# A causal-attention and ternary-FFN layer: wider and later turning of the row maxima, another order in the last projection, and weights rounded between a rope pair's products and sums

## The chip, the cores and the metric

The kernel runs on one core of one Trainium2 chip. The time is that of the device, in microseconds (us), from one launch to its end; lower is better. The names of the engines in what follows: PE is TensorE (matrix products), PEld its weight loads, DVE is VectorE, ACT is ScalarE, POOL is GpSimd, and SP (SyncE) issues the transfers.

## What is computed

For x of 8 batches x 512 tokens x 512 features, all in float32:

```
xn = layernorm(x)
q, k, v = xn @ Wq.T, xn @ Wk.T, xn @ Wv.T            # 16 heads of 32
q, k = rope(q), rope(k)
scores = q @ k.T / sqrt(32), causal
s = softmax(scores) @ v @ Wo.T
bitlinear(x, w) = absmax_quant(layer_norm(x)) @ (sign(round(w / gamma)) * gamma).T,  gamma = mean(|w|) (+ eps)
g = silu(bitlinear(gelu(bitlinear(xn, w_fc)), w_proj))   # 512 -> 2048 -> 512
out = x + s * g
```

## The kernel before

Each engine has one program, written out by hand, and semaphores join them; nothing is reordered by a scheduler. The batches run one after the other. In a batch PE does, in this order: the v products; the q and k products in four pairs (`qk`, L429); the output projection of the batch before; the 16 up-products of the FFN (L555); 44 rounds of scores; and last the 16 heads with transposed scores (L662), and the products with v (L681, `weigh`).

**The rounds.** A round is a row tile and one, two or four heads. `score_round` writes the scores into a PSUM bank (L534) and adds the causal mask (L541). DVE takes the row maxima (L1150), POOL (in the first rounds DVE) makes the bias, ACT takes exp with its row sum (L862). Rounds 4, 15, 26 and 37 hold four heads of the first row tile: there DVE subtracts the maxima (L1158), ACT takes exp (L854), and DVE sums two rounds later (L1164). Five PSUM banks go round, so round r waits until round r-5 has been summed (for round 26: until L1164, which round 31 waits for). Between the rounds PE does the down-products of the FFN (L600), and late output projections. How many is set by `GIVEN` (`FIRST_GIVEN` in batch 0), a table worked out from `EXP_COLS`, which counts 400 columns more for each round in `LSE_AFTER`. The down-products are six halves (h = 0 to 5) in banks 7, 5, 6, 7, 5, 6, and a last one in bank 7 (L611). ACT copies each half out (L875).

**The maxima.** While the second half of the heads is still in its rounds, DVE works out log-sum-exp of the first half (`lse_from_guess`, four steps of three small operations, one after each round in `LSE_AFTER`) and splits it in three f16 parts in `max_parts`, 24 columns for each row tile. After round `TURN_AFTER` PE transposes it (`turn_lse`, L574, four transposes) into the bank of down half `turned_in`; after round `MAX_COPY_AFTER` DVE copies it to `maxT` (L1078, which counts `maxT_ready`); SP moves it into three rows of `q_stack` (L364), and head 0 of the last stage waits for it (`max_dma`). The same happens for the other half of the heads in the last stage, after head 4's scores. The product that next uses the bank waits for `maxT_ready`. In the kernel before, `turned_in` is 6 in batch 0 and 5 in the other batches:

```python
if h == turned_in:
    pe.wait_ge(maxT_ready, 2 * b + 1)
...
if turned_in == N_HALF:
    pe.wait_ge(maxT_ready, 2 * b + 1)
```

**The first batch.** The weights of the FFN are made ternary on the way: the sum of magnitudes of each matrix (`absolute_sum` on DVE, L979, `sum_magnitudes` on ACT, L762), added over partitions by PE (`add_magnitudes`, L415), scales (`ffn_scales`), rounding in 16 units (`round_weights`, L953), turning by PE (`turn_weights`, L400) and keeping by ACT (`keep_weights`, L738 and L741). Rope on DVE has, for each pair, four products (L1126) and two sums (L1132). Hidden activations are made by L831 (gelu), L1172 and L1174.

**The end.** In the last batch `last_out_projection` (L467) makes the projection of the four token tiles after the last group of heads; `finish_context` (L1239, L1241) on DVE gives it that group, `finish_gate` (L1245) makes the gate, and `scale_by_gate` multiplies (L1086) and adds x (L1091).

Of the kernel before, what the change touches and what calls it, by code (L numbers as in the profile page):

```python
# [33 lines left out]
LSE_AFTER = {27: 0, 29: 1, 31: 2, 33: 3}  # L34
TURN_AFTER = 36
MAX_COPY_AFTER = 37
# [39 lines left out]
ABS_ACT = 3  # L76
# [33 lines left out]
def program(nc, x, w_q, w_k, w_v, w_o, w_fc, w_proj, rope_cos, rope_sin, out, norm_row):  # L110
    with ExitStack() as ctx:
# [32 lines left out]
        max_parts = mix[:, 0, 64:160].bitcast(F16).rearrange("p (a i s h) -> p a i s h", a=2, i=NT, s=SPLITS)  # L144
# [116 lines left out]
        TURNS_AFTER_QK = [[8, 9], [10, 11], [], [], fu[0:2], fu[2:3], fu[3:4], fu[4:5]]  # L261
        TURNS_IN_UP = {0: fu[5:7], 1: fu[7:8], 2: fu[8:10], 3: fu[10:11], 4: fu[11:12], 6: fu[12:13], 7: fu[13:14], 8: fu[14:15], 9: fu[15:16]}
        MADE_AFTER_ROPE = [fu[0:2], fu[2:5], fu[5:8], fu[8:12]]
        MADE_AFTER_UP = {3: fu[12:13], 4: fu[13:14], 5: fu[14:15], 6: fu[15:16]}
        PROJ_SUMS_BEFORE_ROPE = [(), (0, 1, 2), (3, 4), ()]
        KEPT_BEFORE_ROPE = [[], fu[0:2], fu[2:5], []]
        KEPT_IN_UP = {0: fu[5:7], 1: fu[7:8], 2: fu[8:10], 3: fu[10:11], 4: fu[11:12], 6: fu[12:13], 7: fu[13:14], 8: fu[14:15], 9: fu[15:16]}
# [120 lines left out]
        def _(pe):  # L388
# [82 lines left out]
            def last_out_projection(b):  # L471

                pe.wait_ge(ctx_lo, b * NG + NG - 1)
                for t in range(NT):
                    last_out_products(b, t, range(1 if t < NT - 1 else 0, NG - 1))
                pe.wait_ge(ctx_lo, b * NG + NG)
                for t in range(NT):
                    last_out_products(b, t, range(NG - 1, NG)).then_inc(wo_ps, 1)

            def body(b, first=False, last=False):  # L480
# [17 lines left out]
                for pair in range(4):  # L498
                    if pair >= 2:
                        pe.wait_ge(rope_prod_ready, b * 16 + 4 * (pair - 2) + 4)  # L500
                    if first:
                        pe.wait_ge(w_kept, ND + 2 * pair + 2)
                    for half in range(2):
                        three_products(banks[:, 2 + 2 * (pair % 2) + half, :],
                                       lambda a, r, c: (qkT[:, pair // 2, r, c, pair % 2, half, :], xT[:, a, c, :]),
                                       ND, "qk").then_inc(qk_ps, 1)
                        for u in TURNS_AFTER_QK[2 * pair + half] if first else []:
                            turn_weights(u, u + 1)
                        if first and (pair, half) == (1, 0):
# [34 lines left out]
                for f in range(FC):  # L544
# [12 lines left out]
                    mm.then_inc(fc_ps, 1)  # L557
                    for u in TURNS_IN_UP.get(f, []) if first else []:
                        turn_weights(u, u + 1)
                    if first and f == 0:  # L560
                        add_magnitudes(1)
# [8 lines left out]
                def turn_lse(half, bank):  # L570

                    pe.wait_ge(lse_split, 2 * b + half + 1)
                    for i in range(NT):
                        mm = pe.transpose(banks16[0:SPLITS * HH, bank, i * P:(i + 1) * P],  # L574
                                          max_parts[:, half, i].rearrange("p s h -> p (s h)"), ident16[:])
                    mm.then_inc(maxT_ps, 1)
# [152 lines left out]
        def _(act):  # L729
# [57 lines left out]
            def body(b, first=False, last=False):  # L787
# [15 lines left out]
                for pair in range(3):  # L803
                    for k in PROJ_SUMS_BEFORE_ROPE[pair] if first else []:
                        sum_magnitudes(1, k)
                    for n, u in enumerate(KEPT_BEFORE_ROPE[pair] if first else []):
                        keep_weights(u)
                        if pair == 2 and n == 1:
                            for k in range(5, N_ABS):
                                sum_magnitudes(1, k)  # L810
                    for u in OUT_KEPT_BEFORE_ROPE[pair] if b == 1 else []:
                        keep_weights(u)
                    split_rotated(pair)

# [87 lines left out]
        def _(dve):  # L902
# [79 lines left out]
            def first_weights():  # L982
# [21 lines left out]
                for k in range(ABS_ACT, N_ABS - 2):  # L1004
                    absolute_sum(k)
# [7 lines left out]
                for k in range(N_ABS - 2, N_ABS):  # L1013
                    absolute_sum(k)
                total_magnitudes(0)
# [98 lines left out]
            def body(b, first=False, last=False):  # L1114
# [4 lines left out]
                for pair in range(4):  # L1119
# [10 lines left out]
                    dve.wait_ge(rope_prod_ready, b * 16 + 4 * pair + 4)  # L1130
                    for half, op in enumerate((ALU.subtract, ALU.add)):
                        nc.vector.tensor_tensor(rope_sum[:, pair % 2, half, :], rope_prods[:, 2 * half, :], rope_prods[:, 2 * half + 1, :],  # L1132
                                                op).then_inc(rope_sum_ready, 1)
                    if pair == 0 and first:
                        ffn_scales(0)
                    if pair == 3 and first:
                        total_magnitudes(1)
                        ffn_scales(1)
# [109 lines left out]
                for g in range(NG):  # L1248
                    if g == 1 and not last:
                        normalise(b + 1)  # L1250
                    finish_context(g)
# [8 lines left out]
                for t in range(NT):  # L1260
                    finish_gate(t)
# [174 lines left out]
```

## Time and profile before

| | |
|---|---|
| time, median of 3 runs | 1143.91 us (1142.93 to 1144.2) |
| the profiled execution | 1143.62 us, span of its instructions 1141.9 us |
| granted TensorE clock, mean | 0.999 |
| busy: PE, DVE, ACT, POOL | 1104.4, 854.7, 793.4, 506.8 us |
| share of the chain that ended last | PE 86%, DVE 9%, ACT 3% |

The span runs from the first to the last instruction; the 1.7 us between it and the profiled time lie around it. PE is busy for 97% of the span, and a time saved on another engine counts only where PE waits for that engine.

### The profile page before, as it was taken

The numbers are of one execution on the slowest core, as the hardware profiler recorded it, in microseconds if no ns is written. First come the engines' busy times: TensorE is split into PE (matmuls) and PEld (weight loads), VectorE is DVE, ScalarE is ACT, GpSimd is POOL, SyncE is SP. The second block draws the span as 40 slices with busy tenths as digits, with TensorE's granted clock in tenths as the row PEclk, the third lists the DMA queues.
The fourth block names the chain that finished last, engine by engine and source line by source line (L and its number), as shares of the span: only waits on it lengthen the run. The fifth ranks groups of instructions, "written<-read, shape, count | busy, mean of one in ns | idle before, by whom it ended". The sixth has DMA issues, their size and how long they took to land.

```text
span 1141.9 us, 20209 instructions
## 1 busy us (share of the span) xinstructions
PE 1104.4 (97%) x7548; PEld 606.0 (53%) x7548; DVE 854.7 (75%) x1596; ACT 793.4 (69%) x1508; POOL 506.8 (44%) x915
## 2 busy tenths in 40 slices
PE   4989999999999999999999999999999999999997
PEld 3555654457444674446644475445744467444753
DVE  7997877798558986489756986479855897658964
ACT  4788884588835878269863798448882687727984
POOL 2135361563616635265433745156361653527533
PEclk9999999999999999999999999999999999999999
DMA  8391002920019101381016410192011910145111
GB/s 312 158 111 39 2 3 65 109 79 19 3 37 156 38 2 30 44 123 38 3 29 78 89 38 4 29 110 84 11 15 38 144 38 2 30 56 74 38 40 38
DMA packets 52610, 67.30 MB, mean 59 GB/s; under 512 B 9376, under 2 KB 34336, under 8 KB 52000
## 3 DMA queue, kind: packets, MB, share of 16 engines
q1 hardware_dynamic: 52512, 66.02, 31.4%
q8 instruction: 59, 0.97, 0.4%
q14 instruction: 39, 0.32, 0.1%
HBM read 31.98 MB, written 8.40 MB: 35 GB/s over the span
## 4 chain that ended last, share of the span: by engine, by line
PE 86%; DVE 9%; ACT 3%; issue 1%; DMA 1%; SPq 0%; POOL 0%; DVEq 0%
PE banks L429 21%; PE banks L555 19%; PE banks L600 11%; PE banks L662 7%; PE banks L681 7%; PE banks L534 5%; PE banks L611 5%; PE banks L446 5%; DVE mix L1150 2%; PE banks L541 2%; ACT banks L862 1%; PE banks L460 1%; DVE arena L1126 1%; PE banks L467 1%; DMA v_sb<-in_L_attn_Wv_dram 1%
## 5 line engine op out<-in xcount | busy, mean ns | idle before, releaser
L862 ACT ACTIVATE banks<-banks,mix,scl 128x384 f32<-128x384 f32 (+2 forms) x384 | 248.0, 648 | 26.9 <-POOL mix L1359 22.0
L1150 DVE TENSOR_REDUCE mix<-banks 128x1 f32<-128x512 f32 (+3 forms) x352 | 216.9, 636 | 34.2 <-PE banks L541 31.1
L555 PE MATMUL banks<-xT,fcT 128*128 128x512 f16 x1024 | 227.7, 379 | 2.1 <-ACT xh_buf L826 2.0
L600 PE MATMUL banks<-proj_ones,arena 128*128 128x256 f16 (+1 forms) x1536 | 214.4, 273 | 4.2 <-DVE mix L1078 4.2
L885 ACT ACTIVATE arena<-banks,scl 128x1280 f32<-128x1280 f32 x128 | 163.1, 1329 | 31.9 <-PE banks L662 29.0
L1350 POOL TENSOR_TENSOR xh_buf<-xh_buf 128x512 f32<-128x512 f32 x120 | 152.6, 1272 | 70.5 <-ACT xh_buf L826 69.2
L429 PE MATMUL banks<-xT,qkT 128*128 128x512 f16 x768 | 168.7, 379 | 0.0
L600 PEld LDWEIGHTS banks<-proj_ones,arena 128*128 128x128 f16 x1536 | 141.2, 97 | 41.6 <-issue 5.9
L555 PEld LDWEIGHTS banks<-xT,fcT 128*128 128x128 f16 x1024 | 98.5, 98 | 121.5 <-ACT xh_buf L826 6.8
L1359 POOL TENSOR_SCALAR mix<-mix,scl 128x1 f32<-128x1 f32 (+1 forms) x288 | 77.2, 268 | 183.3 <-DVE mix L1150 182.0
L1126 DVE TENSOR_TENSOR arena<-banks,mix 128x512 f32<-128x512 f32 x128 | 79.4, 682 | 93.6 <-PE banks L429 93.6
L831 ACT ACTIVATE banks<-banks,scl 128x512 f32<-128x512 f32 x128 | 84.8, 663 | 76.5 <-PE banks L555 75.3
L1344 POOL TENSOR_TENSOR xh_buf<-xr_buf,xh_buf 128x512 f16<-128x512 f32 x32 | 37.2, 1185 | 221.6 <-ACT xh_buf L801 221.6
L534 PE MATMUL banks<-stacks 96*128 96x384 f16 (+3 forms) x512 | 127.8, 300 | 4.5 <-DVE mix L1164 2.7
L1384 POOL TENSOR_SCALAR_AFFINE_SELECT arena<-arena 128x256 f32<-128x256 f32 x256 | 106.4, 444 | 43.0 <-ACT arena L885 39.6
L429 PEld LDWEIGHTS banks<-xT,qkT 128*128 128x128 f16 x768 | 74.9, 98 | 87.8
L1172 DVE TENSOR_SCALAR arena<-banks,scl 128x512 f16<-128x512 f32 x128 | 95.8, 748 | 27.3 <-ACT banks L831 26.5
L1174 DVE SCALAR_TENSOR_TENSOR arena<-banks,scl,arena 128x512 f16<-128x512 f32 x128 | 96.1, 751 | 4.5
L662 PE MATMUL banks<-stacks 99*128 99x512 f16 (+3 forms) x512 | 91.2, 301 | 0.0
L826 ACT ACTIVATE xh_buf<-banks,scl 128x512 f32<-128x512 f32 x128 | 87.3, 682 | 5.1 <-DVE arena L1174 3.2
L681 PE MATMUL banks<-arena,v_sb 128*32 128x512 f32 (+3 forms) x1024 | 87.0, 441 | 0.2 <-POOL arena L1384 0.2
L541 PE MATMUL banks<-mask_q,ident 128*128 128x128 bf16 (+2 forms) x352 | 85.8, 244 | 0.0
(165 smaller groups left out, 1450.8 us busy)
## 6 DMA issues: line engine op xcount, KB each, us to landing
stacks<-xh_buf SPq DMA_DIRECT2D x96, 128.0 KB, 5.2
stacks<-split_buf SPq DMA_DIRECT2D x96, 128.0 KB, 6.9
out_dram<-arena SPq DMA_DIRECT2D x32, 256.0 KB, 2.0
xr_buf<-in_L_attn_x_dram SPq DMA_DIRECT2D x7, 1024.0 KB, 9.9
resid<-in_L_attn_x_dram SPq DMA_DIRECT2D x28, 256.0 KB, 5.6
stacks<-in_L_ffn_w_fc_dram SPq DMA_DIRECT2D x1, 4096.0 KB, 25.4
arena<-in_L_ffn_w_proj_dram SPq DMA_DIRECT2D x1, 4096.0 KB, 15.3
mix<-norm_row SPq DMA_DIRECT2D x8, 256.0 KB, 4.9
```

Source lines behind the costliest of these rows:

```text
L429: mm = pe.matmul(out_ap, lhs, rhs, start=(c == 0 and k == 0), stop=(c == n - 1 and k == 2))
L534: pe.matmul(bank[:, k * keys:(k + 1) * keys], q_stack[0:KS, h0 + k, i * P:(i + 1) * P], k_stack[0:KS, h0 + k, 0:keys], start=(k == 0), sto ...
L541: pe.matmul(diagonal, ident16[:], mask, start=False, stop=True).then_inc(s_ps, 1)
L555: mm = pe.matmul(banks[:, UP_BANKS[f % NUB], :], fcT[:, c, f * P:(f + 1) * P], xT[:, part, c, :], start=(c == 0 and part == 0), stop=(c == ...
L600: mm = pe.matmul(banks[:, DOWN_BANKS[h % 3], 0:cols.stop - cols.start], hid[:, part, f, t * P:(t + 1) * P], proj_ones[:, f, cols], start=( ...
L662: mm = pe.matmul(ps[:, at:at + n], k_stack[0:KM, h, j * P:(j + 1) * P], q_stack[0:KM, h, j * P:S], start=True, stop=True)
L681: mm = pe.matmul(banks[k * DK:(k + 1) * DK, 6 + g % 2, j * P:S], v_sb[:, j, head * DK:(head + 1) * DK], probs[:, g % 2, k, at:at + n], sta ...
L862: mm = nc.scalar.activation(block, block, ACT.Exp, scale=col(EXP_SCALE), bias=exp_bias[:, i, h0 + k:h0 + k + 1], accum_out=row_sum[:, i, h ...
L885: nc.scalar.activation(probs[:, g % 2, h % GH, :], st_region[h % 2][:, 0:PROBS], ACT.Exp, scale=col(EXP_SCALE)).then_inc(probs_ready, 1)
L1150: nc.vector.tensor_reduce(row_max[:, i, h0:h0 + n], scores_of(r), AX_X, ALU.max).then_inc(max_ready, 1)
L1350: nc.gpsimd.tensor_tensor(sq_sum[:], sq_sum[:], squares[f % NSQ], ALU.add).then_inc(sq_added, 1)
L1384: nc.gpsimd.affine_select(blocks, blocks, [[0, 2], [1, P]], ALU.is_ge, 0.0, base=0, channel_multiplier=-1).then_inc(probs_masked, 1)
```

## The change

Four things are changed.

1. **Turning of the maxima, every batch.** `LSE_AFTER`, `TURN_AFTER` and `MAX_COPY_AFTER` move by one or two rounds, and `max_parts` moves to another place of `mix`, so that each transpose reads 128 columns (its own 24 and what stands behind them) in place of 24. `turned_in` becomes 6 in every batch. `GIVEN` is worked out from the new table.
2. **Last projection.** PE finishes tiles 0 and 1 before it starts tiles 2 and 3, and DVE finishes the gate before the last group's context in place of after it.
3. **First batch, DVE.** Units of weights are rounded between a pair's products and its sums; one of the five absolute sums of w_fc that DVE did goes to ACT; totals are taken behind the sums of pair 0, and ahead of those of pair 3.
4. **First batch, PE and ACT.** Units are turned and kept somewhat later.

```diff
-LSE_AFTER = {27: 0, 29: 1, 31: 2, 33: 3}
-TURN_AFTER = 36
-MAX_COPY_AFTER = 37
+LSE_AFTER = {28: 0, 30: 1, 32: 2, 34: 3}
+TURN_AFTER = 38
+MAX_COPY_AFTER = 39
-ABS_ACT = 3
+ABS_ACT = 4
-        max_parts = mix[:, 0, 64:160].bitcast(F16).rearrange("p (a i s h) -> p a i s h", a=2, i=NT, s=SPLITS)
+        parts_f = mix[:, 1, 304:452].bitcast(F16)
+        max_parts = parts_f[:, 0:8 * SPLITS * HH].rearrange("p (a i s h) -> p a i s h", a=2, i=NT, s=SPLITS)
-        TURNS_AFTER_QK = [[8, 9], [10, 11], [], [], fu[0:2], fu[2:3], fu[3:4], fu[4:5]]
+        TURNS_AFTER_QK = [[8, 9], [10, 11], [], [], [], fu[0:1], fu[1:3], fu[3:5]]
-        MADE_AFTER_ROPE = [fu[0:2], fu[2:5], fu[5:8], fu[8:12]]
+        MADE_BEFORE_SUMS = [[], fu[0:2], fu[3:5], fu[6:8]]
+        MADE_AFTER_ROPE = [[], fu[2:3], fu[5:6], fu[8:12]]
@@ last_out_projection
-                for t in range(NT):
-                    last_out_products(b, t, range(1 if t < NT - 1 else 0, NG - 1))
+                for t in range(2):
+                    last_out_products(b, t, range(1, NG - 1))
                 pe.wait_ge(ctx_lo, b * NG + NG)
-                for t in range(NT):
+                for t in range(2):
                     last_out_products(b, t, range(NG - 1, NG)).then_inc(wo_ps, 1)
+                for t in range(2, NT):
+                    last_out_products(b, t, range(1 if t < NT - 1 else 0, NG)).then_inc(wo_ps, 1)
@@ turn_lse
-                        mm = pe.transpose(banks16[0:SPLITS * HH, bank, i * P:(i + 1) * P],
-                                          max_parts[:, half, i].rearrange("p s h -> p (s h)"), ident16[:])
+                        at = (half * NT + i) * SPLITS * HH
+                        mm = pe.transpose(banks16[:, bank, i * P:(i + 1) * P], parts_f[:, at:at + P], ident16[:])
@@ first_weights (DVE)
-                for k in range(ABS_ACT, N_ABS - 2):
+                for k in range(ABS_ACT, N_ABS - 1):
                     absolute_sum(k)
 ...
-                for k in range(N_ABS - 2, N_ABS):
-                    absolute_sum(k)
-                total_magnitudes(0)
+                absolute_sum(N_ABS - 1)
@@ body (DVE)
+                    for u in MADE_BEFORE_SUMS[pair] if first else []:
+                        round_weights(u)
+                    if pair == 3 and first:
+                        total_magnitudes(1)
                     for half, op in enumerate((ALU.subtract, ALU.add)):
 ...
                     if pair == 0 and first:
+                        total_magnitudes(0)
                         ffn_scales(0)
                     if pair == 3 and first:
-                        total_magnitudes(1)
                         ffn_scales(1)
@@ last part of the batch (DVE)
+                    if g == NG - 1 and last:
+                        for t in range(NT):
+                            finish_gate(t)
                     finish_context(g)
 ...
-                for t in range(NT):
+                for t in range(0 if last else NT):
                     finish_gate(t)
```

On PE the place is rounds 37 to 39 of batch 1, the same in batches 2 to 7 (batches are counted from 0). `stacks` are the scores of a round, `mask_q` their mask, `proj_ones` the down-products (256 or 257 columns by half), `ident,mix` the turning of the maxima. Before, with the last down-products of round 36 as the first row:

```order
L600 MATMUL banks<-proj_ones,arena 128x256 x10
L574 MATMUL banks<-ident,mix 24x128 x4
L534 MATMUL banks<-stacks 128x128 x4
L541 MATMUL banks<-mask_q,ident 128x512
L600 MATMUL banks<-proj_ones,arena 128x256 x8
L534 MATMUL banks<-stacks 128x384
L541 MATMUL banks<-mask_q,ident 128x128
L600 MATMUL banks<-proj_ones,arena 128x256 x2
L600 MATMUL banks<-proj_ones,arena 128x257 x4
L534 MATMUL banks<-stacks 128x384
```

And in the changed kernel:

```order
L606 MATMUL banks<-proj_ones,arena 128x256 x6
L540 MATMUL banks<-stacks 128x128 x4
L547 MATMUL banks<-mask_q,ident 128x512
L606 MATMUL banks<-proj_ones,arena 128x256 x12
L540 MATMUL banks<-stacks 128x384
L547 MATMUL banks<-mask_q,ident 128x128
L606 MATMUL banks<-proj_ones,arena 128x256 x2
L606 MATMUL banks<-proj_ones,arena 128x257 x2
L581 MATMUL banks<-ident,mix 128x128 x4
L540 MATMUL banks<-stacks 128x384
```

The turning stood ahead of round 37, with 10 down-products between it and half 5 (the first row of 257 columns at this place), which uses its bank. Now it stands ahead of round 39, after half 5 has begun, in the bank that only the last product (L611 before) uses again, and its output has 128 rows in place of 24.

On DVE the place is the same batch from round 26 (`128x4` with the subtraction behind it) on. Before:

```order
L1150 TENSOR_REDUCE mix<-banks 128x4
L1158 TENSOR_TENSOR banks<-banks,mix 128x512
L1150 TENSOR_REDUCE mix<-banks 128x1
L1056 TENSOR_TENSOR mix<-mix 128x32
L1057 TENSOR_SCALAR mix<-mix 128x32
L1058 TENSOR_SCALAR mix<-mix 128x32
L1150 TENSOR_REDUCE mix<-banks 128x1
L1164 TENSOR_REDUCE mix<-banks 128x4
L1150 TENSOR_REDUCE mix<-banks 128x1
```

And in the changed kernel:

```order
L1163 TENSOR_REDUCE mix<-banks 128x4
L1171 TENSOR_TENSOR banks<-banks,mix 128x512
L1163 TENSOR_REDUCE mix<-banks 128x1 x2
L1177 TENSOR_REDUCE mix<-banks 128x4
L1065 TENSOR_TENSOR mix<-mix 128x32
L1066 TENSOR_SCALAR mix<-mix 128x32
L1067 TENSOR_SCALAR mix<-mix 128x32
L1163 TENSOR_REDUCE mix<-banks 128x1 x2
```

The three small operations of the first step stood ahead of round 28's maxima and of the sum of round 26 (`128x4`, L1164 before); now they stand behind both.

On DVE at the end of the program, before (`ctxT` is the last group's context, `gate_sum` the gate, `arena` the result):

```order
L1239 CAST ctxT<-banks 128x512
L1241 TENSOR_TENSOR ctxT<-banks,ctxT 128x512
L1245 SCALAR_TENSOR_TENSOR gate_sum<-xr_buf,gate_sum 128x512 x4
L1086 SCALAR_TENSOR_TENSOR arena<-banks,gate_scale,gate_sum 128x512 x2
L1091 TENSOR_TENSOR arena<-arena,xh_buf 128x512
```

And in the changed kernel:

```order
L1258 SCALAR_TENSOR_TENSOR gate_sum<-xr_buf,gate_sum 128x512 x4
L1252 CAST ctxT<-banks 128x512
L1254 TENSOR_TENSOR ctxT<-banks,ctxT 128x512
L1095 SCALAR_TENSOR_TENSOR arena<-banks,gate_scale,gate_sum 128x512 x2
L1100 TENSOR_TENSOR arena<-arena,xh_buf 128x512
```

The four operations of the gate changed places with the two of the context. On PE the 39 products at this end are the same in number, in another order of tiles.

## Rows read from the trace of the kernel before

**Rows 1.** The page, chain that ended last, shares of the span by engine.

```profile
PE 86%; DVE 9%; ACT 3%; issue 1%; DMA 1%; SPq 0%; POOL 0%; DVEq 0%
```

**Rows 2.** Waits of the whole span: us in total, times, longest.

```profile
PE banks L600 <- DVE mix L1078: 4.2, 7, 0.6
PE banks L534 <- DVE mix L1164: 2.7, 8, 1.1
```

**Rows 3.** Timeline of PE, batch 1: start, length, instructions [idle before <-releaser].

```profile
271.36 0.60 PE L600 MATMUL banks<-proj_ones,arena 128*128 128x256 f16 x4
272.19 0.39 PE L534 MATMUL banks<-stacks 96*128 96x256 f16 x2 [0.22 <-DVE mix L1164]
...
280.34 0.38 PE L600 MATMUL banks<-proj_ones,arena 128*128 128x256 f16 x2
...
281.32 0.60 PE L600 MATMUL banks<-proj_ones,arena 128*128 128x257 f16 x4 [0.60 <-DVE mix L1078]
```

**Rows 4.** Timeline of ACT and DVE, batch 1, rounds 26 to 28.

```profile
269.49 0.66 ACT L854 ACTIVATE banks<-banks,scl 128x512 f32<-128x512 f32 x1
...
269.83 0.18 DVE L1056 TENSOR_TENSOR mix<-mix 128x32 f32<-128x32 f32 x1
...
270.98 0.56 DVE L1150 TENSOR_REDUCE mix<-banks 128x1 f32<-128x384 f32 x1
...
271.45 0.68 DVE L1164 TENSOR_REDUCE mix<-banks 128x4 f32<-128x512 f32 x1
```

**Rows 5.** The chain in order of time, batch 1: start, us, work.

```profile
277.43 1.10 PE banks L600 x10
...
295.65 0.55 PE banks L662 x4
...
296.64 0.32 PE banks L574 x4
296.96 0.65 PE banks L662 x4
```

**Rows 6.** The same view, batch 0.

```profile
24.87 0.45 PE banks L403 x8
```

**Rows 7.** Groups by line and shape, weight loads of two kinds of transposes.

```profile
L403 PEld LDWEIGHTS banks<-ident,split_buf 128*128 128x128 f16 x96 | 7.1, 109 | 4.4 <-DVE split_buf L919 2.8 <-issue 0.2
...
L574 PEld LDWEIGHTS banks<-ident,mix 128*24 128x24 f16 x64 | 3.4, 92 | 5.1 <-issue 5.1
```

**Rows 8.** Timeline of batch 1, stage of the heads.

```profile
291.43 7.55 ACT L885 ACTIVATE arena<-banks,scl 128x1280 f32<-128x1280 f32 x6 [2.84 <-PE banks L662]
...
297.10 0.41 DVE L1078 COPY mix<-banks 24x512 f16<-24x512 f16 x1 [3.40 <-PE banks L574]
...
301.84 0.49 PEld L662 LDWEIGHTS banks<-stacks 99*128 99x128 f16 x4 [0.20 <-issue]
```

**Rows 9.** Timeline of the end of the program.

```profile
1123.22 2.55 ACT L892 ACTIVATE xr_buf<-gate_sum,gate_scale 128x512 f32<-128x512 f32 x4
...
1127.01 8.59 PE L467 MATMUL banks<-voT,ctxT 128*128 128x512 f16 x39
1127.15 0.69 DVE L1239 CAST ctxT<-banks 128x512 f16<-128x512 f32 x1 [2.85 <-PE banks L681]
...
1128.48 2.49 DVE L1245 SCALAR_TENSOR_TENSOR gate_sum<-xr_buf,gate_sum 128x512 f32<-128x512 f32 x4
...
1137.89 0.75 DVE L1086 SCALAR_TENSOR_TENSOR arena<-banks,gate_scale,gate_sum 128x512 f32<-128x512 f32 x1
```

**Rows 10.** Timeline of batch 0, projections.

```profile
42.15 2.34 DVE L979 TENSOR_REDUCE ln<-stacks 128x1 f32<-128x1024 f32 x2
...
47.95 1.22 ACT L801 CAST xh_buf<-xr_buf 128x512 f16<-128x512 f32 x2 [2.56 <-DVE xr_buf L1132]
...
71.09 0.16 DVE L937 TENSOR_SCALAR scl<-banks 128x1 f32<-128x1 f32 x1 [0.47 <-PE banks L415]
...
78.76 1.90 PE L555 MATMUL banks<-xT,fcT 128*128 128x512 f16 x8 [1.61 <-ACT xh_buf L826]
```

More of the change, by code:

```diff
@@ L260, in program @@
         TURNS_AFTER_V = [[4], [5], [6], [7]]
-        TURNS_AFTER_QK = [[8, 9], [10, 11], [], [], fu[0:2], fu[2:3], fu[3:4], fu[4:5]]
-        TURNS_IN_UP = {0: fu[5:7], 1: fu[7:8], 2: fu[8:10], 3: fu[10:11], 4: fu[11:12], 6: fu[12:13], 7: fu[13:14], 8: fu[14:15], 9: fu[15:16]}
-        MADE_AFTER_ROPE = [fu[0:2], fu[2:5], fu[5:8], fu[8:12]]
+        TURNS_AFTER_QK = [[8, 9], [10, 11], [], [], [], fu[0:1], fu[1:3], fu[3:5]]
+        TURNS_IN_UP = {0: fu[5:6], 1: fu[6:7], 2: fu[7:9], 3: fu[9:10], 4: fu[10:11], 5: fu[11:12],
+                       6: fu[12:13], 7: fu[13:14], 8: fu[14:15], 9: fu[15:16]}
+        MADE_BEFORE_SUMS = [[], fu[0:2], fu[3:5], fu[6:8]]
+        MADE_AFTER_ROPE = [[], fu[2:3], fu[5:6], fu[8:12]]
         MADE_AFTER_UP = {3: fu[12:13], 4: fu[13:14], 5: fu[14:15], 6: fu[15:16]}
-        PROJ_SUMS_BEFORE_ROPE = [(), (0, 1, 2), (3, 4), ()]
-        KEPT_BEFORE_ROPE = [[], fu[0:2], fu[2:5], []]
-        KEPT_IN_UP = {0: fu[5:7], 1: fu[7:8], 2: fu[8:10], 3: fu[10:11], 4: fu[11:12], 6: fu[12:13], 7: fu[13:14], 8: fu[14:15], 9: fu[15:16]}
+        PROJ_SUMS_BEFORE_ROPE = [(), (0, 1, 2, 3), (4,)]
+        KEPT_BEFORE_ROPE = [[], fu[0:1], fu[1:3]]
+        PROJ_SUMS_AFTER_KEPT = [(), (), (5,)]
+        KEPT_IN_UP = {0: fu[6:7], 1: fu[7:8], 2: fu[8:9], 3: fu[9:10], 4: fu[10:11], 5: fu[11:12], 6: fu[12:13], 7: fu[13:14], 8: fu[14:15], 9: fu[15:16]}
         OUT_TURNS_AFTER_QK = [[], ou[0:1], ou[1:2], ou[2:3], ou[3:4], [], [], []]
@@ L508, in body @@
                             turn_weights(u, u + 1)
-                        if first and (pair, half) == (1, 0):
+                        if first and (pair, half) == (1, 1):
                             add_magnitudes(0)
@@ L557, in body @@
                     mm.then_inc(fc_ps, 1)
+                    if first and f == 1:
+                        add_magnitudes(1)
                     for u in TURNS_IN_UP.get(f, []) if first else []:
                         turn_weights(u, u + 1)
-                    if first and f == 0:
-                        add_magnitudes(1)
                     if FC - EARLY <= f < FC - 1:
@@ L805, in body @@
                         sum_magnitudes(1, k)
-                    for n, u in enumerate(KEPT_BEFORE_ROPE[pair] if first else []):
+                    for u in KEPT_BEFORE_ROPE[pair] if first else []:
                         keep_weights(u)
-                        if pair == 2 and n == 1:
-                            for k in range(5, N_ABS):
-                                sum_magnitudes(1, k)
+                    for k in PROJ_SUMS_AFTER_KEPT[pair] if first else []:
+                        sum_magnitudes(1, k)
                     for u in OUT_KEPT_BEFORE_ROPE[pair] if b == 1 else []:
@@ L813, in body @@
                     split_rotated(pair)
+                if first:
+                    keep_weights(fu[3])
+                    for k in (6, 7):
+                        sum_magnitudes(1, k)
+                    keep_weights(fu[4])
+                    keep_weights(fu[5])
                 nc.scalar.preload_act_table(ACT.Gelu)
```

## The prediction, made before the changed kernel ran

> **What bounds the kernel now.** I read the chain that ended last first. PE holds 86% of the span in it [rows 1], so the question is where PE waits, and where it is slowed without a wait. The list of waits gives the first: among PE's waits two come back once in nearly every batch, one of 0.60 us for DVE's copy of the turned maxima (L1078, 7 times) and one for the sum of a four-head round (L1164, 8 times) [rows 2]. The timeline then shows what each really costs. Down-products follow each other every 0.11 us (10 in 1.10) [rows 5]. The two that start at 280.34 would let the next start at 280.56; it starts at 281.32: 0.76 us lost. The four that start at 271.36 would let round 31 start at 271.80; it starts at 272.19: 0.39 us lost [rows 3]. Batches 2 to 7 show the same two places with the same waits. Last, the chain in order of time shows work that takes longer than it should: after the turning of the maxima four score products hold 0.65 us, and 0.55 a head earlier, and the four transposes themselves hold 0.32 [rows 5].
>
> **The two waits of a round (change 1).** The bank of the turned maxima was that of down half 5, which came 10 down-products and two rounds after them. Now it is bank 7, which nothing uses until the last product after all rounds, so the wait of 0.76 us goes, in batches 1 to 7 (batch 0 had that bank already). The 0.39 us go if the sum of round 26 is ready by 271.80. DVE began the first log-sum-exp step at 269.83 and came to round 28's maxima only at 270.98 (0.56), then to the sum (0.68) [rows 4]. Without the step in between, the maxima run from 269.8 to 270.4, and the sum, whose input ACT had ready at 269.49 + 0.66 = 270.15 [rows 4], from 270.4 to 271.1: 0.7 us ahead of need. The step then runs where the sum was; DVE's work in the rounds is the same in sum, so all that follows on DVE is no later than before. Sum: 7 x (0.76 + 0.39) = 8.05 us. Below it the bound is nothing, if other waits take their place (a rival, below); above it there is none, since the waits can't give more than they cost.
>
> **The width of the transposes (change 1).** Four transposes of 128 columns at full pace take half of what eight take: 0.45 / 2 = 0.22 us, and behind those eight the v products come without delay [rows 6]. The turning holds 0.32, and the products behind it 0.10 more than usual [rows 5]: 0.20 us for each turning. I put this down to the 24-column weights, which seem not to be loaded beside the products ahead. There are 16 turnings; the first of batch 0 lies where DVE is behind, so 15 x 0.20 = 3.0 us. From below: no gain, and four loads each dearer by 109 - 92 = 17 ns [rows 7], 64 in all: 1.1 us lost. I take the 3.0, since the transposes of [rows 6] are of the same type and the very width that the change brings. A rule speaks against it. The Trainium skill (TensorE: Matmul & The Clock Gate, LDWEIGHTS) says that a load's time goes with its number of columns, about P / 1.2 ns; by it a load of 24 columns should take 20 ns and one of 128 107 ns, and 64 loads would cost 5.6 us more if nothing hid them. The trace doesn't bear it out for the narrow one: 92 ns against 109 [rows 7].
>
> **The last projection (change 2).** The 39 products begin at 1127.01 and take 0.22 us each [rows 9]. Before, the first tile was whole after 30 of them, at 1133.6, and DVE then had four tiles one behind the other and came to the last scaling at 1137.89 [rows 9]. Now tile 0 is whole after 15 (1130.3), tile 1 after 18, tile 2 after 27 (1132.9) and tile 3 after 39 (1135.6). With some 1.5 us of DVE's work for a tile, tiles 0 to 2 are done by about 1134.8, and the last scaling starts at 1135.75: 2.1 us earlier. The gate now stands ahead of the last context on DVE. It takes 2.49 us, and DVE waited 2.85 us ahead of the context's 1127.15, since 1124.3; the last tanh ends at 1123.22 + 2.55 = 1125.77 [rows 9], so the gate ends at about 1127.0 and fits. Were it late, the context would be too, but PE has 12 products (2.6 us) to do before it needs it, 1.2 us more than the context takes. So 2.1 us; bounds 1.5 and 2.3.
>
> **The first batch (changes 3 and 4).** DVE's two absolute sums of w_fc behind the rope rows, 2.34 us, become one: 1.17 us less [rows 10], at a place where PE and ACT both wait for DVE (1.61 us of PE's at 78.76, 2.56 of ACT's at 47.95) [rows 10]. The sum that ACT takes over costs it about as much, and that wait of 2.56 us covers it. The exchange over PE for the total (0.47 us idle of DVE at 71.09) [rows 10] goes for w_proj, where sums now stand in between, and comes for w_fc, which had the products of pair 0 in between: no change. Rounding between products and sums moves the same 12 units about, none is added; the units that are turned later were waiting for DVE before. Cover is the idle time of PE at 78.76; if it's gone, a turned unit costs PE some 1 us. I take 1.0 us of the 1.17, bounds 0 and 1.6. In the rounds of batch 0 DVE is the one that is behind, and there the copy (0.41 us, as in [rows 8]) no longer stands ahead of the sum of round 37: 0.4 us.
>
> **The sum.** 8.05 + 3.0 + 2.1 + 1.0 + 0.4 = 14.55 us. The profiled execution took 1143.62 us (span 1141.9, and 1.7 around it), so 1129.1; the median of the runs shown is 0.3 above it: **1129.3 us**.
>
> **Will the gain be kept?** At the end of the rounds ACT had waited 2.84 us for head 0's scores [rows 8]; with PE some 1.35 us earlier it still waits 1.5, so PE stays the one that decides. In the stages behind, everything hangs on PE's pace and moves with it.
>
> **Rivals.**
>
> A. *Other waits take the place of the two.* PE arrives earlier at rounds 32 to 41, while the banks come free by ACT's sums, which hang on DVE's maxima, and those come no earlier. For it: the room before each such bank is small, and the products between the rounds, which make it, now alternate (2, 4, 2, 4 of the counted pairs). Against it: no other wait of PE in the rounds of batches 1 to 7 is in the list. If half of 8.05 comes back, 1133.3; if all, 1137.4.
>
> B. *The wide transposes bring nothing, or cost.* The 0.20 us could come from the turning itself or from the f16 output. Then the sum loses 3.0 to 4.1: 1132.3 to 1133.4. By the Trainium skill's rule on loads, named above, it would be 1137.9.
>
> C. *Slower: the rows of maxima reach head 0 too late.* The copy of the first half now comes two rounds later, near 282, and SP's transfer must land before head 0's scores, which start 0.7 us ahead of 291.43 - 1.35, at 289.3: 7 us of room. For the second half the copy starts at 297.10 and PE begins head 8 with them at 301.84 [rows 8], so 4.7 us are enough. It would take a landing 2.1 us later than the room, 9 us, in all 8 batches to undo the 14.55 us and lose 0.2% (2.3 us); a landing after 10 us gives 1129.3 + 8 x 2.9 = 1152.
>
> D. *PE was not held by these waits:* what it gains it gives back ahead of the heads, in the wait for ACT's last sums. Then only the turnings and the tail could count, and, with the former lost too, the time stays within 0.2%. Against it stand the 2.84 us of ACT.
>
> **Numbers.** Main case 0.57, A 0.24, B 0.12, C 0.04, D 0.03. The range takes in the main case with its bounds (1128.5 with all upper ones, and 1.1 less if the longest wait for the sum, 1.1 us in batch 0 [rows 2], goes as well), B, and A to somewhat over half: 1127 to 1136. About 0.2%, 2.3 us, is what a measurement of this kernel can tell from no change. Faster 0.93, same 0.03, slower 0.04.
>
> **What would show it.** In the profile after: no wait of PE for the copy of the maxima and none for the sum of round 26 in batches 1 to 7; the four transposes at 0.22 us in the chain with 0.55 behind them; a batch shorter by 1.55 us; the last scaling 2.1 us nearer to PE's last part; the first hidden activation 1 us earlier. The prediction is wrong if PE shows new waits for ACT or DVE in rounds 32 to 41, or ahead of head 0; if the transposes still hold 0.32; or if rounding ahead of the sums delays the transfers of the rotated pairs so that the first scores wait.

## The result, and the profile after

| | before | changed |
|---|---|---|
| median | 1143.51 us (4 runs) | 1127.11 us (4 runs, 1124.74 to 1128.03) |
| ratio | | 0.9853, 95% interval 0.9836 to 0.9870 |
| the profiled execution | 1143.62 us, span 1141.9 | 1127.08 us, span 1125.4 |

The ratio is 16.8 us of 1143.51; the forecast was 14.6 us. By it the time is 1126.7 us, a little below the lower end of the range (1127.0), while the median itself is a little above it. So the direction and nearly all terms were right, and one was too small.

The page of the changed kernel, the chain that ended last, shares of the span by engine, which answers to [rows 1]:

```profile
PE 92%; DVE 3%; ACT 2%; POOL 1%; DMA 1%; issue 1%; SPq 0%; DVEq 0%; POOLq 0%
```

DVE went from 9% to 3% of it. In the waits of the changed kernel (us, times, longest) neither of [rows 2] is left for PE. Behind the opening one (12.5 us) and one of 2.1 us at 13.2 us, which stand in both kernels, the largest waits of its matmuls are these:

```profile
PE banks L561 <- ACT xh_buf L837: 2.7, 1, 2.7
...
PE banks L540 <- ACT banks L873: 2.0, 4, 0.8
```

The 2.7 us are new in size ([rows 10] had 1.61 at the same place, up-product 3 of batch 0). The others are the four of batch 0, where the kernel before had four too.

The chain in order of time, batch 1 of the changed kernel: the last down-products ahead of the first turning, the turning (L581) and the down-products behind it; then a head's scores ahead of the second turning, that turning and the scores behind it.

```profile
276.60 0.44 PE banks L606 x4
277.04 0.22 PE banks L581 x4
277.48 0.89 PE banks L606 x8
...
291.22 0.55 PE banks L668 x4
...
292.20 0.22 PE banks L581 x4
292.42 0.55 PE banks L668 x4
```

Against [rows 5] the four transposes hold 0.22 us in place of 0.32, and the scores behind them 0.55 in place of 0.65: 0.20 us for each turning, as forecast. The timelines show the weight loads of that second turning, first in the kernel before, then in the changed one:

```profile
296.57 0.22 PEld L574 LDWEIGHTS banks<-ident,mix 128*24 128x24 f16 x4 [0.43 <-issue]
```

```profile
291.82 0.43 PEld L581 LDWEIGHTS banks<-ident,mix 128*128 128x128 f16 x4
...
292.04 0.38 PE L581 MATMUL banks<-ident,mix 128*128 128x128 f16 x4
```

The down-products ahead end at 296.64 before and at 292.20 after. So the narrow loads began 0.07 us before that end, together with the transposes themselves (296.57), and the wide ones 0.38 us before it.

A measure for each batch is the first of the 32 products of one column behind the rounds (L635 before, L641 after). It starts at 149.27 us in batch 0 and at 1096.58 in batch 7 of the kernel before, and at 146.17 and 1082.52 in the changed one. Batch 0, in the kernel before and in the changed one:

```profile
149.27 0.94 PE L635 MATMUL banks<-ones,arena 128*128 128x1 f16 x32
```

```profile
146.17 0.94 PE L641 MATMUL banks<-ones,arena 128*128 128x1 f16 x32
```

So batch 0 gave 3.10 us up to there, the seven periods between them 14.06 - 3.10 = 10.96 us (forecast 10.85), and what lies behind it 16.5 - 14.06 = 2.4 us (forecast 2.1 and 0.2 of a turning). The middle and the end are as forecast; batch 0, where I had 1.4, is not. The measure of batch 0 carries the opening of the program with it, which differs by up to 1.2 us between profiled executions whose edits lie behind it. The periods between batches don't: from the third one on they are 134.92 us before and 133.37 after, each within 0.01 us.

The end of the program, timeline of the changed kernel, for [rows 9]:

```profile
1109.94 2.49 DVE L1258 SCALAR_TENSOR_TENSOR gate_sum<-xr_buf,gate_sum 128x512 f32<-128x512 f32 x4
...
1112.75 8.59 PE L471 MATMUL banks<-voT,ctxT 128*128 128x512 f16 x39
1112.88 0.69 DVE L1252 CAST ctxT<-banks 128x512 f16<-128x512 f32 x1 [0.45 <-PE banks L687]
...
1116.30 1.41 DVE L1095 SCALAR_TENSOR_TENSOR arena<-banks,gate_scale,gate_sum 128x512 f32<-128x512 f32 x2 [2.01 <-PE banks L471]
...
1121.38 0.75 DVE L1095 SCALAR_TENSOR_TENSOR arena<-banks,gate_scale,gate_sum 128x512 f32<-128x512 f32 x1 [0.90 <-PE banks L471]
```

The gate ends 0.45 us ahead of the context, and the last scaling comes 8.63 us behind PE's first product there, in place of 10.88: 2.25 us.

Batch 0, stretches of the changed kernel's time: us, then busy time of PE, PEld, DVE, ACT and POOL with instructions, granted TensorE clock, DMA share, GB/s.

```profile
70.00:72.00 2.00, 1.95 (x17) 1.67 (x15) 1.31 (x2) 2.00 (x5) 1.39 (x2) 1.00 1.15 116
72.00:74.70 2.70, 0.03 (x1) 0.03 (x2) 2.59 (x5) 1.42 (x3) 1.33 (x1) 1.00 1.25 73
74.70:78.00 3.30, 3.30 (x9) 1.23 (x10) 2.05 (x3) 2.08 (x3) 1.14 (x1) 0.51 1.17 124
```

PE sat idle for 2.7 us, and then the clock was granted at 0.51, the lower of its two levels (1.2 GHz), for 3.3 us. The length of the wait alone doesn't tell when this happens: a wait of 2.08 us that ended at 15.3 us, in both kernels, left the clock at 1.00. The eight products of up-product 3 show it in the timeline:

```profile
74.67 3.53 PE L561 MATMUL banks<-xT,fcT 128*128 128x512 f16 x8 [2.72 <-ACT xh_buf L837]
```

They took 3.53 us where the same eight took 1.90 in [rows 10]. Up-product 3 began 4.09 us earlier than before (78.76), and 1.6 us of that went to the clock. The run at 1124.74 us has a mean clock of 1.0 in place of 0.998.

Where did 4.09 us come from, when I had forecast 1.0 for the whole of changes 3 and 4? The groups of the 16 roundings, before:

```profile
L953 DVE TENSOR_SCALAR ctxT<-arena,scl 128x1024 f32<-128x1024 f32 x4 | 5.2, 1324 | 0.0
...
L953 DVE TENSOR_SCALAR gate_sum<-stacks,scl 128x1024 f32<-128x1024 f32 x4 | 4.4, 1122 | 0.0
...
L953 DVE TENSOR_SCALAR gate_sum<-arena,scl 128x1024 f32<-128x1024 f32 x4 | 3.8, 974 | 0.0
L953 DVE TENSOR_SCALAR ctxT<-stacks,scl 128x1024 f32<-128x1024 f32 x4 | 3.7, 973 | 0.0
```

and in the changed kernel:

```profile
L964 DVE TENSOR_SCALAR ctxT<-arena,scl 128x1024 f32<-128x1024 f32 x4 | 3.4, 862 | 0.7 <-PE banks L404 0.7
L964 DVE TENSOR_SCALAR ctxT<-stacks,scl 128x1024 f32<-128x1024 f32 x4 | 3.4, 876 | 0.2
L964 DVE TENSOR_SCALAR gate_sum<-arena,scl 128x1024 f32<-128x1024 f32 x4 | 2.9, 747 | 0.0
L964 DVE TENSOR_SCALAR gate_sum<-stacks,scl 128x1024 f32<-128x1024 f32 x4 | 2.9, 746 | 0.0
```

The same 16 operations took 17.1 us before and 12.6 after. The timeline of before shows which were slow: those beside a subtraction of POOL.

```profile
55.77 2.32 DVE L953 TENSOR_SCALAR ctxT<-stacks,scl 128x1024 f32<-128x1024 f32 x2
55.99 3.13 POOL L1344 TENSOR_TENSOR xh_buf<-xr_buf,xh_buf 128x512 f16<-128x512 f32 x2 [5.06 <-ACT xh_buf L801]
58.02 1.64 DVE L953 TENSOR_SCALAR gate_sum<-stacks,scl 128x1024 f32<-128x1024 f32 x1
...
64.03 1.41 DVE L953 TENSOR_SCALAR ctxT<-stacks,scl 128x1024 f32<-128x1024 f32 x2
...
67.28 2.72 POOL L1344 TENSOR_TENSOR split_buf<-xr_buf,split_buf 128x512 f16<-128x512 f32 x2 [8.16 <-ACT split_buf L801]
67.93 2.61 DVE L1132 TENSOR_TENSOR xr_buf<-arena 128x512 f32<-128x512 f32 x2
```

With POOL quiet (64.03) two roundings take 1.41 us; beside it one alone takes 1.64. The two rope sums at 67.93 take 2.61 us beside POOL. That was in the trace that I had, and I read it as a fixed duration.

The sum of DVE's work up to its first operation on hidden activations (L1172 at 76.44 before, L1185 at 72.36 after: 4.08 us) is this. Less: the 12 roundings ahead of it take 9.7 us in place of 12.75 (3.0; the rest of the 4.5 lies behind it), pair 3's rope sums 1.28 in place of 2.61 (1.3), the sum that went to ACT 1.1, and one small operation of the scales 0.18 in place of 0.82 (0.6). More: new waits of 0.47 for the total of w_fc, 0.70 more for that of w_proj, 0.69 for a turned unit and 0.17 for ACT, 2.0 in all. Three of the rows, from the timeline of the changed kernel:

```profile
65.13 1.28 DVE L1145 TENSOR_TENSOR xr_buf<-arena 128x512 f32<-128x512 f32 x2
67.58 0.16 DVE L948 TENSOR_SCALAR scl<-banks 128x1 f32<-128x1 f32 x1 [1.17 <-PE banks L419]
...
71.12 1.21 DVE L964 TENSOR_SCALAR ctxT<-arena,scl 128x1024 f32<-128x1024 f32 x1 [0.69 <-PE banks L404]
```

### The profile page after: what moved, and what is told of

Same layout as the page of the kernel before. It is cut to its first block, busy times and chain, and to the rows that moved or that the text cites. A ratio compares the mean times of both kernels' runs of the same rounds, so it can differ in the third digit from the quotient of the medians.

```text
span 1125.4 us, 20210 instructions
## 1 busy us (share of the span) xinstructions
PE 1100.0 (98%) x7548; PEld 609.2 (54%) x7548; DVE 843.7 (75%) x1595; ACT 791.3 (70%) x1510; POOL 503.7 (45%) x915
## 4 chain that ended last, share of the span: by engine, by line
PE 92%; DVE 3%; ACT 2%; POOL 1%; DMA 1%; issue 1%; SPq 0%; DVEq 0%; POOLq 0%
PE banks L433 23%; PE banks L561 20%; PE banks L606 14%; PE banks L687 7%; PE banks L668 7%; PE banks L540 6%; PE banks L450 5%; PE banks L617 4%; PE banks L547 2%; ACT banks L873 2%; PE banks L464 1%; PE banks L404 1%; PE banks L471 1%; DVE mix L1163 1%; DMA v_sb<-in_L_attn_Wv_dram 1%
## 5 line engine op out<-in xcount | busy, mean ns | idle before, releaser
L1185 DVE TENSOR_SCALAR arena<-banks,scl 128x512 f16<-128x512 f32 x128 | 95.9, 749 | 29.7 <-ACT banks L842 29.1
```

## Experiments

Each was timed in five rounds against the kernel before on the same chip. A gain in us is 1 less the ratio, times the time before.

**Change 1 alone** (`turning_only`).

```diff
-LSE_AFTER = {27: 0, 29: 1, 31: 2, 33: 3}
-TURN_AFTER = 36
-MAX_COPY_AFTER = 37
+LSE_AFTER = {28: 0, 30: 1, 32: 2, 34: 3}
+TURN_AFTER = 38
+MAX_COPY_AFTER = 39
...
+        parts_f = mix[:, 1, 304:452].bitcast(F16)
...
+                        mm = pe.transpose(banks16[:, bank, i * P:(i + 1) * P], parts_f[:, at:at + P], ident16[:])
```

> The kernel before with change 1 alone (later steps, later and wider turning). Theory (two waits and the narrow loads go, PE paces): 7 x 1.55 + 0.4 in batch 0's rounds = 11.3 us less, 1132.3; each batch from 2 on shorter by 1.56 us. Rival (the gain of the whole change came from elsewhere, or needs the first batch's changes): less than 8 us.

Measured: 1132.58 us, ratio 0.9902 (0.9888 to 0.9915), 11.2 us. The theory holds; most of the change's gain is here. A batch is shorter by 1.55 us (133.37 against 134.92), and the measure of batch 0 comes 0.64 us earlier (148.63).

**Its three parts, one by one.** Only the width (`wide_only`):

```diff
-        max_parts = mix[:, 0, 64:160].bitcast(F16)...
+        parts_f = mix[:, 1, 304:452].bitcast(F16)
...
-                        mm = pe.transpose(banks16[0:SPLITS * HH, bank, i * P:(i + 1) * P], ...
+                        mm = pe.transpose(banks16[:, bank, i * P:(i + 1) * P], parts_f[:, at:at + P], ident16[:])
```

> The kernel before with transposes of 128 columns in place of 24, and nothing else. Theory (0.10 us ahead of and 0.10 behind each turning is the price of the narrow loads): 15 to 16 turnings x 0.20 = 3.0 to 3.2 us less where PE paces; the first turning of a batch stands ahead of the wait for DVE's copy, which may take its part back: 1140.5 to 1142. Rival (the width is of no account or a wide load is dearer): 1143.5 to 1144.6.

Measured: 1141.34 us, 0.9977 (0.9968 to 0.9986), 2.6 us; a batch takes 134.52 us, 0.40 less. The changed kernel with the width alone undone (`narrow_after`, the same diff reversed):

> The changed kernel with transposes of 24 columns as before, and nothing else changed back. Theory: 15 x 0.20 = 3.0 us more than the changed kernel, 1130.1. Rival (width of no account): 1127.1.

Measured: 1129.66 us, 0.9877 (0.9863 to 0.9890). Against the 0.9853 of the changed kernel, 2.7 us more by the ratios, though the intervals of the two (each against before) overlap a little. The periods are sharper: 133.77 us against 133.37, 0.40 for two turnings. Both runs say that the narrow transposes cost what the chain showed, 0.20 us a turning. The edit also gives the output 128 rows and moves `max_parts`; no run parts these from the width of the weights. In the waits of this kernel the weight loads' idle time of [rows 7], 5.1 us in 16 pieces, is back in the same size:

```profile
PEld banks L579 <- issue: 5.1, 16, 0.4
```

Only the place of the turning and the copy (`turn_later_only`):

```diff
-TURN_AFTER = 36
-MAX_COPY_AFTER = 37
+TURN_AFTER = 38
+MAX_COPY_AFTER = 39
```

> The kernel before with the turning and its copy two rounds later, the steps of the log-sum-exp where they were, narrow transposes. Theory: the wait of PE for the copy goes, 7 x 0.76 = 5.3 us, and the 0.39 us for the sum of round 26 stays: 1138.2. Rival (the two waits stand for each other: the one left grows): 1140 or more.

Measured: 1138.74 us, 0.9955 (0.9942 to 0.9967), 5.1 us; a batch takes 134.16 us, 0.76 less. The wait for the copy is no longer in the list, and that for the sum of round 26 stands as it did in [rows 2]:

```profile
PE banks L534 <- DVE mix L1164: 2.7, 8, 1.1
```

Only the steps (`lse_only`). `GIVEN` and the bank of the turning in batch 0 are worked out from this table, so they move with it:

```diff
-LSE_AFTER = {27: 0, 29: 1, 31: 2, 33: 3}
+LSE_AFTER = {28: 0, 30: 1, 32: 2, 34: 3}
```

> The kernel before with the steps of the log-sum-exp one round later and nothing else. Theory: the 0.39 us for the sum of round 26 go, 7 x 0.39 = 2.7 us, and the turning, which now has two rounds in place of three behind the last step, doesn't wait: 1141.3. Rival (the wait for the copy grows by what the other gives): 1144.

Measured: 1141.32 us, 0.9978 (0.9969 to 0.9987), 2.5 us. The time is that of the theory, but by luck. The wait for the sum is gone; the one for the copy stays, with one long case in it and one short wait of a turning for the last step:

```profile
PE banks L600 <- DVE mix L1078: 3.0, 8, 1.9
...
PE banks L574 <- DVE mix L1070: 0.5, 1, 0.5
```

The long case is in batch 0; the other seven are short. Timeline of this kernel, batch 0 and batch 1:

```profile
147.01 0.82 PE L600 MATMUL banks<-proj_ones,arena 128*128 128x257 f16 x6 [1.92 <-DVE mix L1078]
...
282.88 1.48 PE L600 MATMUL banks<-proj_ones,arena 128*128 128x256 f16 x12
...
284.96 0.38 PE L600 MATMUL banks<-proj_ones,arena 128*128 128x257 f16 x2 [0.15 <-DVE mix L1078]
```

In batch 1 `GIVEN` now puts 14 down-products between the turning and half 5 (12 here, 2 behind the next round) in place of 10, and the wait for the copy falls from 0.60 to 0.15 us. So a batch takes 134.08 us, 0.84 less: 0.39 for the sum and 0.45 for the copy, 5.96 us over the seven periods. In batch 0 no down-product stands between the turning and the half in its bank. PE waits 0.55 and 1.92 us there, and the granted clock is 0.53 from 148 to 151 us. Batch 0 ends 4.48 us later for it (1.2 of them are from the opening). The mean clock was 0.997 in 9 of the 11 runs, against 0.998 to 0.999 before.

One by one the three parts shorten a batch by 0.40 + 0.76 + 0.84 = 2.00 us, together by 1.55. The two waits overlap by the 0.45 of the copy. That 2.6 + 5.1 + 2.5 = 10.2 us of the whole times comes near the 11.2 is only because `lse_only` loses in batch 0 what it gains too much in the others. What the two waits give together is seen in `narrow_after`: 134.92 - 133.77 = 1.15 us a batch, the 0.76 + 0.39 of the forecast.

**Change 2 alone** (`tail_only`), the diff of the last projection and of `finish_gate` as shown with the change.

> The kernel before with change 2 alone (order of the last projection, gate ahead of the last context). Theory: last scaling 2.1 us earlier relative to PE's last part, 1141.4. Rival (the stores at the end decide): less than 1 us.

Measured: 1141.82 us, 0.9981 (0.9972 to 0.9990), 2.2 us, as forecast.

**Changes 3 and 4 alone** (`first_only`): the changed kernel with changes 1 and 2 undone.

> The kernel before with changes 3 and 4 alone (first batch). Theory (what I left out is that rounding no longer runs beside POOL's subtractions, so that DVE's 16 roundings take 12.6 us in place of 17.1): PE's stages of batch 0 come 2.3 us earlier, up to 3.9 if the clock doesn't fall in the wait ahead of up-product 3: 1141.2, down to 1139.6. Rival (only the absolute sum that went to ACT counts, as I forecast): 1142.5.

Measured: 1141.04 us, 0.9975 (0.9966 to 0.9984), 2.9 us, against the 1.0 of my forecast (1.4 with the rounds, whose 0.4 belongs to change 1). In the profile batch 0 gives 2.42 us. The clock fell here too: up-product 3 waited 2.73 us and took 3.58.

**Rounding put back behind the sums** (`round_late`).

```diff
-        MADE_BEFORE_SUMS = [[], fu[0:2], fu[3:5], fu[6:8]]
-        MADE_AFTER_ROPE = [[], fu[2:3], fu[5:6], fu[8:12]]
+        MADE_BEFORE_SUMS = [[], [], [], []]
+        MADE_AFTER_ROPE = [[], fu[0:3], fu[3:6], fu[6:12]]
```

> The changed kernel, with the units rounded behind the sums of each pair again; all else as changed. Theory (contention with POOL): the roundings of pairs 1 to 3 run beside POOL's subtractions again and take some 4 us more in all, of which PE sees 1.5 to 3: 1129 to 1130. Rival (the place of the rounding is of no account, only the sum on ACT and the timetable of turning are): 1127, as the changed kernel.

Measured: 1129.24 us, 0.9874 (0.9860 to 0.9887), 2.4 us more than the changed kernel by the ratios, whose intervals overlap. The time is as the theory said, but not for its reason: the 16 roundings took 11.6 us, less than in the changed kernel. ACT came later to the cast that frees POOL: POOL started 3.6 us behind pair 1's sums in place of 0.1 in the kernel before, and now ran beside pair 2's rope sums. Timeline of this kernel, last the wait ahead of pair 3's sums:

```profile
55.71 2.73 POOL L1360 TENSOR_TENSOR xh_buf<-xr_buf,xh_buf 128x512 f16<-128x512 f32 x2 [6.54 <-ACT xh_buf L807]
...
56.65 2.35 DVE L1145 TENSOR_TENSOR xr_buf<-arena 128x512 f32<-128x512 f32 x2
...
65.28 0.16 DVE L938 TENSOR_REDUCE w_all<-ln 128x1 f32<-128x8 f32 x1 [1.79 <-ACT resid L768]
```

The sums took 2.35 us; in the changed kernel they take 1.28, and there POOL runs beside the rope products, which read PSUM and take 2.48 us with or without it, and beside one rounding (1.26). So it isn't the rounding's place as such that counts but what POOL meets, and what DVE has to do while it waits. Counted from the same operation (the rope rows, 40.61 here and 41.12 in the changed kernel) the first hidden activation comes 2.0 us later. The sums beside POOL are 1.1 of it; the wait for ACT's sums of w_proj, 1.79 us in place of 0.17, is 1.6; and a longer wait for a turned unit is 0.45. The faster roundings give back 1.0, and a shorter wait for the total 0.1. In the changed kernel two roundings fill the time in which DVE here waits for ACT.

**POOL kept away from the roundings** (`pool_waits`), all else as before.

```diff
                         pool.wait_ge(rot_hi_ready, b * 8 + 2 * pair + half + 1)
+                        if first:
+                            pool.wait_ge(w_unit_ready, n_first + (2, 5, 8, 12)[pair])
```

> The kernel before, but in batch 0 POOL starts the subtraction of each rope pair only when DVE has rounded the units that stand beside it (2, 5, 8 and 12 of them). Theory (roundings beside POOL's subtractions are slowed): the 16 roundings take about 12 us in place of 17.1, the first hidden activation comes 3 to 4 us earlier, and the time falls by 1 to 3 us, to 1141 to 1143, if the fall of the clock takes some back. Rival (the slow roundings have another cause, such as the transfer of w_proj): roundings stay at 17 us and the time at 1144 or more.

Measured: 1139.81 us, 0.9968 (0.9955 to 0.9980). This line alone, which only makes POOL wait, gives 3.7 us where changes 3 and 4 together gave 2.9, though the intervals overlap. PE had no wait ahead of up-product 3 in this profile, and it took 1.89 us. Groups and timeline of this kernel:

```profile
L953 DVE TENSOR_SCALAR ctxT<-arena,scl 128x1024 f32<-128x1024 f32 x4 | 4.4, 1102 | 0.2 <-PE banks L400 0.2
L953 DVE TENSOR_SCALAR gate_sum<-arena,scl 128x1024 f32<-128x1024 f32 x4 | 3.2, 828 | 0.0
L953 DVE TENSOR_SCALAR gate_sum<-stacks,scl 128x1024 f32<-128x1024 f32 x4 | 2.9, 750 | 0.0
L953 DVE TENSOR_SCALAR ctxT<-stacks,scl 128x1024 f32<-128x1024 f32 x4 | 2.8, 747 | 0.0
```

```profile
55.22 1.41 DVE L953 TENSOR_SCALAR ctxT<-stacks,scl 128x1024 f32<-128x1024 f32 x2
56.55 0.75 DVE L953 TENSOR_SCALAR gate_sum<-stacks,scl 128x1024 f32<-128x1024 f32 x1
57.44 2.29 POOL L1346 TENSOR_TENSOR xh_buf<-xr_buf,xh_buf 128x512 f16<-128x512 f32 x2 [3.41 <-DVE gate_sum L953]
```

13.3 us in place of 17.1: the three roundings that took 2.32 + 1.64 us beside POOL take 1.41 + 0.75 ahead of it, and POOL's two take 2.29 in place of 3.13. The slow rope sums at 67.93 became fast as well (1.29). The slowest roundings left (up to 1.63 us) come behind 82 us, beside POOL's work on the hidden activations (L1352). The rival of another cause falls.

**Only the fourth absolute sum on ACT** (`abs_only`).

```diff
-ABS_ACT = 3
+ABS_ACT = 4
...
-                        if first and (pair, half) == (1, 0):
+                        if first and (pair, half) == (1, 1):
                             add_magnitudes(0)
...
-                for k in range(N_ABS - 2, N_ABS):
-                    absolute_sum(k)
-                total_magnitudes(0)
+                absolute_sum(N_ABS - 1)
...
+                        total_magnitudes(0)
                         ffn_scales(0)
```

> The kernel before with the fourth absolute sum of w_fc on ACT, and the first total and its addition on PE where the changed kernel has them; units are rounded and turned as before. My forecast for the first batch: 1.0 us less than before, 1143.0. Rival (this edit is the whole gain of the first batch): 1141.0.

Measured: 1142.59 us median, 0.9984 (0.9974 to 0.9993), 1.8 us, with runs from 1138.99 to 1143.68. The interval, 0.8 to 3.0 us, holds my forecast for this edit (1.0) and its rival (2.9) alike. The profiled one took 1139.4 us, near the low end; its roundings took 15.4 us in all, and its up-product 3 started at 75.10, 3.66 us earlier than before. What POOL meets seems to change from run to run. That is argued, not shown; only one of these runs has a profile.

**Filling PE's idle time** (`fill_idle`). The 16 products are read by nobody.

```diff
+                    for k in range(16 if first and f == 2 else 0):
+                        pe.matmul(banks[:, 5, 128:512], ident16[:], xT[:, 0, 0, 0:384], start=True, stop=True)
```

> The changed kernel with 16 products of 384 columns that nobody reads, put where PE sat idle for 2.7 us ahead of up-product 3 of batch 0 (their results are not used). Theory (that idle time made the granted clock fall to 0.5 for 3.3 us, which cost 1.7 us): no fall, 1125.4, near the one run of the changed kernel that was at 1124.74. Rival (the clock fell for another reason, or the stage is held by DVE anyway): 1127.1 or later.

Measured: 1125.73 us, 0.9843 (0.9829 to 0.9856). Stretches of this kernel, the same as above:

```profile
72.00:74.70 2.70, 2.70 (x20) 1.78 (x19) 2.63 (x4) 1.41 (x3) 1.90 (x2) 1.00 1.30 81
74.70:78.00 3.30, 3.17 (x20) 1.82 (x19) 2.65 (x5) 3.19 (x5) 0.58 (x1) 1.00 1.14 115
```

The clock stays at 1.00 and up-product 3 takes 1.90 us. It starts at 75.23, 0.56 us later than in the changed kernel, but so does up-product 0, long before the fillers (63.50 against 62.94), so they delayed nothing. The measure behind the rounds of batch 0 comes 1.12 us earlier all the same (145.05 against 146.17), which with the 0.56 makes 1.7 us, about what the eight products had lost to the low clock (1.6). By the ratios 1.1 us are gained, which is less than the intervals can tell apart.

**Fewer fillers, and w_proj's total one up-product earlier** (`best`).

```diff
-                    if first and f == 1:
+                    if first and f == 0:
                         add_magnitudes(1)
+                    for k in range(12 if first and f == 2 else 0):
+                        pe.matmul(banks[:, 5, 128:512], ident16[:], xT[:, 0, 0, 0:384], start=True, stop=True)
```

> The changed kernel with 12 products that nobody reads in PE's idle time ahead of up-product 3 of batch 0, and the addition of w_proj's magnitudes on PE one up-product earlier (their results are not used; the addition's are). Theory: DVE's wait of 1.17 us for that addition becomes 0.5, up-product 3 comes 0.7 us earlier than with the filling alone, and the clock stays: 1125.0. Rival (the stage behind is held by PE's own work, so nothing is added to the filling): 1125.7.

Measured: 1125.80 us, 0.9849 (0.9836 to 0.9862): the same as with the filling alone. DVE no longer waited for the total, but then for a turned unit, so that the first hidden activation came no earlier:

```profile
71.41 1.25 DVE L966 TENSOR_SCALAR ctxT<-arena,scl 128x1024 f32<-128x1024 f32 x1 [1.85 <-PE banks L404]
```

## Why the prediction was right and where it was too small

- **"7 x (0.76 + 0.39) = 8.05 us".** Right. Both waits are gone from the list, and without the width (`narrow_after`) the seven periods are 7.9 us shorter. Apart they gave 5.1 and 2.5 us (5.3 and 2.7 forecast); the first is sound, the second is luck, as told above.
- **"15 x 0.20 = 3.0 us" for the width.** Right in place (0.22 and 0.55 in the chain) and nearly in size: 2.6 and 2.7 us by two runs. The rule of the Trainium skill (TensorE: Matmul & The Clock Gate, LDWEIGHTS), that a load's time goes with its columns, would by my estimate have made this part 5.6 us dearer if nothing hid the loads; the trace of the changed kernel has 97 ns for a load of 128 columns against 92 for one of 24, so it didn't hold here. The same page says elsewhere (Weight-path perf modes) that a load of 128 columns that aren't FP32 is made fast; with that the trace agrees, 97 ns in f16 against 144 for one of 128 columns in f32 (L404 of the changed kernel).
- **The last projection, 2.1 us.** Right: 2.25 us in the profile, 2.2 by its own run. The gate ended 0.45 us ahead of the context; I had said 0.15.
- **Batch 0's rounds, 0.4 us.** With change 1 alone the measure of batch 0 came 0.64 us earlier.
- **"I take 1.0 us of the 1.17, bounds 0 and 1.6": this is the step that failed.** Changes 3 and 4 gave 2.9 us. The sentence behind it, that "rounding between products and sums moves the same 12 units about, none is added", counts operations and takes their time as fixed. But DVE's roundings and rope sums had run beside POOL's subtractions and took about twice as long for it (0.75 and 1.66 us, 1.28 and 2.61). In the changed kernel most of them don't: 3.0 us less for roundings and 1.3 for rope sums ahead of the first hidden activation, a term that I had put at nothing. `pool_waits`, which changes only when POOL works, gave 3.7 us.
- **The exchanges for the totals, "no change".** Wrong too, the other way. The one for w_proj didn't go but grew from 0.47 to 1.17 us, since PE there adds w_proj's magnitudes one up-product later (`best`, which moves them back, has no such wait), and the one for w_fc came with 0.47.
- **The clock.** I didn't count it. It fell in the wait ahead of up-product 3 and took back 1.6 us; without that the forecast would have been further off.
- **Rival A** (other waits in the rounds) didn't occur: seven periods gave 10.96 us. **Rival B** didn't either. **C** and **D** fell: no wait of PE for the rows of maxima is in the list, and the periods kept the gain.

What stays open: how the 2.9 us of changes 3 and 4 are divided between the sum that went to ACT and POOL's neighbours, since `abs_only` alone gave 1.8 with a wide interval; why its runs spread over 4.7 us; and what lets the clock fall behind a wait of 1.92 us and not behind one of 2.08.

## What to carry to other kernels

A duration in a trace holds for its neighbours as well: before moving an operation, compare its shortest and its mean time, and if they differ, look at what another engine did beside the longer instances. When a wait is shortened ahead of an engine whose own idle time grows by it, look at the granted clock behind that idle time too. Weights of few columns between wide ones cost a gap on either side here, which no wait of the products shows; the idle time of the weight loads and the chain's time for each instruction do. When parts of a change are run apart, compare the periods of the batches and not only the whole times: two errors of `lse_only` cancelled in the whole time and stood apart in the periods.

## What the runs showed of the hardware that I hadn't expected

- An operation of DVE with both sides in SBUF runs slower beside one of POOL: a rounding of 128x1024 f32 takes 0.75 us alone and up to 1.66 beside POOL's subtraction; two rope sums 1.28 and 2.61; POOL's pair 2.29 and 3.13. Products that read PSUM took 2.48 us either way.
- After 2.7 us without work PE was granted 0.51 of its clock for 3.3 us, and eight products took 3.53 us in place of 1.90; with fillers in that time the clock stayed. In the kernel before, 1.61 us of idle time at the same place left it at 1.00, and so did 2.08 us at 13.2 us in both kernels. In `round_late` 2.32 us were followed by a clock of 0.57 for 3.2 us, in `lse_only` 0.55 and 1.92 us, close together, by 0.53 for 3 us.
- Loads of 24 columns (92 ns) began 0.07 us before the products ahead ended, and the turning with the products behind it took 0.20 us more; loads of 128 columns (97 ns) began 0.38 us before and cost nothing more.
